# A loop written out: TensorE's stream in a routed expert stage of 79 slots

## The reference, cut to what matters

```python
logits = xt @ Wg.T + bg
top_vals, top_idx = jax.lax.top_k(logits, 2)
rw = softmax(top_vals)
gu = einsum('th,ehf->tef', xt, Wgu) + bgu        # per expert 256 -> 512
gate, up = minimum(gu[..., ::2], 7), clip(gu[..., 1::2], -7, 7)
gated = (up + 1) * gate * sigmoid(1.702 * gate)
out_e = einsum('tef,efh->teh', gated, Wd) + bd   # per expert 256 -> 256
out = einsum('teh,te->th', out_e, onehot(top_idx, rw))
```

## Time and profile before

| | |
|---|---|
| median of three runs | 772.86 us (769.19 to 773.58) |
| the profiled execution | 767.49 us |
| its span, first to last instruction | 765.7 us |
| TensorE busy, share of the span | 613.7 us, 80% |
| weight loads | 314.6 us, 41% |
| VectorE | 488.7 us, 64% |
| ScalarE | 328.9 us, 43% |
| GpSimd | 351.0 us, 46% |
| mean granted TensorE clock | 0.898 |

### The profile page before, as it was taken

One profiled execution on the slowest core, in us unless ns is written; L12 is line 12 of the kernel. 1 busy time (PEld: TensorE's weight loads), 2 busy tenths in 40 slices (PEclk: granted clock), 3 DMA queues, 4 the chain that ended last, 5 costly groups with the idle time before them and its releaser, 6 DMA issues.

```text
span 765.7 us, 13490 instructions
## 1 busy us (share of the span) xinstructions
PE 613.7 (80%) x3148; PEld 314.6 (41%) x3149; DVE 488.7 (64%) x1381; ACT 328.9 (43%) x739; POOL 351.0 (46%) x433
## 2 busy tenths in 40 slices
PE   1987888778999797979798973069999999999910
PEld 0666333523434252525252543034555555555510
DVE  5576325756487566866767644446777777777796
ACT  3854634226666464655555332013333333333331
POOL 5864623232744656467557355412333333333353
PEclk9998987679999899989899985579999999999975
DMA  9811000074000101010101011523333333333397
GB/s 321 272 11 12 0 1 0 2 270 146 1 1 12 49 2 56 4 55 0 55 1 57 1 55 56 168 55 84 91 87 88 85 87 88 86 86 88 73 377 275
DMA packets 93219, 62.37 MB, mean 81 GB/s; under 512 B 68186, under 2 KB 78558, under 8 KB 93056
## 3 DMA queue, kind: packets, MB, share of 16 engines
q1 hardware_dynamic: 85168, 44.04, 20.8%
q0 software_dynamic: 6864, 16.86, 6.5%
q10 hardware_dynamic: 1152, 1.06, 0.5%
HBM read 27.97 MB, written 25.56 MB: 70 GB/s over the span
## 4 chain that ended last, share of the span: by engine, by line
PE 51%; SPq 14%; DVE 12%; issue 9%; ACT 6%; DMA 4%; POOL 2%; another core or an unknown queue 1%; ACTq 0%; POOLq 0%; DVEq 0%
SPq L379 7%; PE bank L1037 5%; PE bank L891 4%; PE bank L866 4%; PE bank L995 3%; PE bank L1017 3%; SPq L380 3%; PE bank L855 3%; PE bank L1054 3%; PE bank L1019 3%; SPq L375 3%; PE bank L1068 2%; PE bank L1160 2%; PE bank L1161 2%; PE bank L1163 2%
## 5 line engine op out<-in xcount | busy, mean ns | idle before, releaser
L588 POOL DMA_INDIRECT y_rows<-AR x79 | 77.2, 977 | 165.4 <-ACT AR L815 161.1
L491 POOL TENSOR_TENSOR W<-STG,W 128x512 f16<-128x512 f32 (+1 forms) x48 | 56.1, 1169 | 122.2 <-ACT W L620 120.9
L804 ACT ACTIVATE AR<-AR 128x256 f32<-128x256 f32 x79 | 32.9, 417 | 160.4 <-DVE AR L1585 138.1
L1410 DVE RECIPROCAL AR<-bank 128x512 f32<-128x512 f32 x16 | 53.7, 3354 | 38.1 <-PE bank L1037 31.2
L548 POOL DMA_INDIRECT xs_rows<-AR,SLOT x64 | 63.4, 991 | 27.4 <-issue 18.1
L720 ACT ACTIVATE AR<-bank 128x512 f32<-128x512 f32 (+1 forms) x80 | 47.6, 596 | 51.9 <-PE bank L1023 47.9
L1396 DVE TENSOR_REDUCE MX<-bank 128x4 f32<-128x308 f32 x128 | 56.6, 475 | 18.4 <-PE bank L995 13.8
L1585 DVE TENSOR_SCALAR AR<-bank 128x256 f32<-128x256 f32 x79 | 33.5, 424 | 51.5 <-PE bank L1163 47.9
L1160 PE MATMUL bank<-W,AR 128*128 x158 | 61.3, 388 | 0.0
L1161 PE MATMUL bank<-W,AR 128*128 x158 | 61.1, 387 | 0.0
L995 PE MATMUL bank<-KCUR,AR 128*128 (+1 forms) x128 | 41.9, 329 | 19.4 <-DVE MX L1396 10.0
(11 more groups left out here) (229 smaller groups left out, 1443.6 us busy)
## 6 DMA issues: line engine op xcount, KB each, us to landing
W<-in_wexp SPq DMA_DIRECT2D x16, 768.0 KB, 5.3
W<-y_rows SPq DMA_DIRECT2D x8, 1024.0 KB, 15.3
X<-in_x SPq DMA_DIRECT2D x4, 1024.0 KB, 11.9
out<-X SPq DMA_DIRECT2D x8, 512.0 KB, 8.1
CST<-in_cst SPq DMA_DIRECT2D x1, 1309.0 KB, 8.4
AR<-xs_rows SPq DMA_TRANSPOSE x79
AR<-xs_rows SPq DMA_DIRECT2D x79, 1.0 KB
y_rows<-AR POOLq DMA_INDIRECT x79
```

The source lines that it names most:

```text
L491: pool.tensor_tensor(w[:, 1], STG[:, q], w[:, 0], ALU.subtract).then_inc(s["w_split"], 1)
L588: pool.indirect_dma_start(y_rows, bass.IndirectOffsetOnAxis(ap=NIX[:, k:k + 1], axis=0), CY[:, k, :], None, bounds_check=TOPK * NTOK - 1, ...
L1410: dve.reciprocal(AT[:, m], DEN[:, :]).then_inc(s["rec_s"], 1)
```

## The change: what it does

TensorE's loop in the expert stage is written out in Python: 79 times `c_tg`, `c_down`, `c_gu` with n a constant, so all waits compare with constants. Each `c_down` and each `c_gu` fetches its expert number with an `expert(n)` of its own, which stands directly ahead of it. `QUAD` is still made but no longer read. Two waits go, in `c_gu` for `cu_r` and in `c_tg` for `cgl_r`; both are implied by other waits ahead of them on TensorE. The other engines' instructions stay as they are.

```diff
             def c_gu(n, k, t, e):
                 q = k % 2
-                if not isinstance(n, int) or n >= 2:
-                    pe.wait_ge(s["cu_r"], n - 1)
                 pe.wait_ge(XTIN[k], 16 * (t + 1))
...
             def c_tg(n, q):
                 pe.wait_ge(s["cgd_r"], n + 1)
-                if not isinstance(n, int) or n >= 2:
-                    pe.wait_ge(s["cgl_r"], n - 1)
                 for c in range(DC):
...
-            def steps(n, t, k, u):
-
-                four = pe.value_load(QUAD[0:1, ds(t, 1)], min_val=0, max_val=NEXP ** 4 - 1)
-                c_tg(n + 1, 1)
-                c_down(n, 0, four % NEXP)
-                c_gu(n + 3, (k + 3) % IN, u + (k + 3) // IN, four // NEXP ** 2 % NEXP)
-                c_tg(n + 2, 0)
-                c_down(n + 1, 1, four // NEXP % NEXP)
-                c_gu(n + 4, k, u + 1, four // NEXP ** 3)
-
-            steps(0, 0, 0, 0)
-            with pe.Fori(0, (NSLOT - 7) // IN) as t:
-                steps(t * IN + 2, t * 2 + 1, 2, t)
-                steps(t * IN + 4, t * 2 + 2, 0, t + 1)
-            c_tg(NSLOT - 4, 1)
-            c_down(NSLOT - 5, 0, expert(NSLOT - 5))
-            c_gu(NSLOT - 2, (NSLOT - 2) % IN, (NSLOT - 2) // IN, expert(NSLOT - 2))
...
+            for n in range(3):
+                c_gu(n, n % IN, n // IN, expert(n))
+                if n == 1:
+                    c_tg(0, 0)
+            for n in range(NSLOT):
+                if n + 1 < NSLOT:
+                    c_tg(n + 1, (n + 1) % 2)
+                c_down(n, n % 2, expert(n))
+                if n + 3 < NSLOT:
+                    c_gu(n + 3, (n + 3) % IN, (n + 3) // IN, expert(n + 3))
```

## The result

The changed kernel takes 798.19 us (median of four runs, 796.96 to 802.15) against 771.03 us (768.92 to 773.58) of the kernel before, run beside it: a ratio of 1.036, 95% interval 1.031 to 1.041. It is slower, as forecast (790.6 us, range 782 to 801), and 7.6 us above the forecast value. The profiled execution took 796.96 us, its span is 795.2 us, 29.5 us more than before.

The account below looks back on a forecast made before the run. It took SyncE's 2.86 us a slot as the floor under the expert stage. Held loads add 17.4 us up to slot 74, then +0.6 and -0.3 at the end: 772.86 + 17.7 = 790.6 us, range 782 to 801.

Parts of the forecast that it names:

- What bounds the kernel: Expert stage before the change: SyncE's transposing loads, 2.86 us a slot, are the floor; a quicker TensorE gains nearly nothing.
- The load is held at the wait: `c_down`'s register load starts only when `c_tg`'s wait for `cgd_r` ends, so `c_down` starts 0.77 us after the release.
- The cycle of two slots: TensorE's expert stage: 2.65 + 0.77 + 1.25 + 1.51 = 6.18 us per two slots, taken as 3.08 us a slot.
- the third term: From the start of `c_down` to the start of `c_gu`: 1.30 us less 0.051 for a dropped wait, 1.25 us.
- the other form that it named: Slots alternate, one long (3.5 us) and the next short (2.7 us), with the same sum for the pair.
- TensorE's busy share: In the expert stage of the changed profile, TensorE would be busy near 2.6 of 3.1 us a slot.
- The start: Slot 7 finds its rows and full clock; counted from slot 1's transposes at 510.81, its `c_gu` starts at 525.15 us.
- The end: Slot 74 to the final additions takes 17.7 us instead of 17.1, +0.6; a wait for `y_rows`' second read goes, -0.3.
- The loads hide: Rival at the wait for `cgd_r`: loads are covered, SyncE's pace holds, about 772.7 us; chance 0.06.
- The clock dips: Rival: TensorE, busy less, runs at 0.93 of the clock in the stage, +7.6 us, about 798 us; chance 0.06.
- Code fetches stall TensorE: Rival: fetching written-out code, 12 to 24 more packets, stalls TensorE 1 us each, 803 to 815 us; chance 0.07.
- The sum: Whole kernel: 17.4 + 0.6 - 0.3 = +17.7 us, giving 790.6 us; own range 785 to 797.

Follow-up runs that it names:

- written-out one with packed numbers: Changed kernel's written-out stream and dropped waits, but with the packed `QUAD` load of every second slot, ahead of `c_tg`: 775.46 us, ratio 1.004.
- The placements: Four variants of the changed kernel with `c_down`'s load, `c_gu`'s load, both, or a single load a slot placed ahead of `c_tg`: ratios between 1.003 and 1.010.
- one load ahead: Changed kernel with one expert load a slot, ahead of `c_tg`, kept in a register from `c_gu` to the same slot's `c_down`: 776.02 us, ratio 1.003.
- constant numbers: Changed kernel with each slot's expert a fixed constant, so no register loads and no routing's choice of weights: 771.24 us, ratio 0.997.
- the kernel with the pause: Changed kernel, with VectorE waiting before its second group of final additions until GpSimd has issued its last scatter: 798.80 us, ratio 1.036.

## Why the prediction was right, and where it was not

**What bounds the kernel: right.** The bound named, SyncE's 2.86 us a slot, is confirmed by taking it away: 2.70 us. The busy share of TensorE (97% of the window in the earlier trace rows) would have said otherwise: matmul lengths overlap (in the earlier trace rows one of 0.38 us starts at 724.54 and the next at 724.76), so a short wait between two need not show as idle time. That this hid the waits for rows is inferred: those listed from slot 8 to 74 are 1.3 us in all, while slot 7 to 74 gained 8.8 us with SyncE written out, about 1.4 of it in the step to slot 8.

**The load is held at the wait: right.** The load starts at 644.6, with the release at 644.61, as the earlier trace rows had it at 720.9 and 727.2. Moving the loads ahead of the wait, with nothing else changed, takes 1.036 to 1.008. This was the step on which the forecast stood. In the traces of the four written-out kernels with `c_down`'s load behind the transposes it starts within 0.01 us of their weight load in about every second slot (32 to 34 times between 525 and 735 us).

**The cycle of two slots: right in form, 0.09 us short.** Forecast 2.65 + 0.77 + 1.25 + 1.51 = 6.18, cut to 6.16. Averaged over the 32 long slots from slot 11 to 74, with the 1.52 of the short ones, it is 2.66 + 0.75 + 1.35 + 1.52 = 6.28. Only the third term, from `c_down` to `c_gu`, was mis-sized, 1.25 for 1.35: I took one case from the earlier trace rows, in which the load takes 0.31 us, and subtracted a wait from it. A load there is not always 0.30 us; over these slots:

```profile
L1147 PEldq TENSOR_LOAD <-AR x133: 296/303/523, 531.6 to 738.8; - x133
```

In the long slots the load ahead of `c_gu` takes 0.43 us on average, and all the others take 0.30 to 0.31; why is open. The three loads of the earlier trace rows showed nothing of it. 3.13 instead of 3.08 us a slot is 3.3 us over 67 slots. The sequencer is not stuck in every slot, as the working had it first, but in every second one (33 of 67), the other form that it named. TensorE's busy share was misjudged: 173.41 of 192 us is 2.83 us of 3.13, not near 2.6.

**The start: partly right.** Slot 7 indeed found its rows, and there was no low clock: 1.00 in the window from 524 us, where before had 0.57. But the stage began later: the first `c_gu` at 503.39 instead of 502.92 us, the second at 507.36 instead of 505.88, after waiting 0.81 us for its rows, and the granted clock was 0.50 from 504 to 508 us and 0.59 to 512, where before had 0.57 and 1.00. So the transposes of slot 1, from which the forecast counted, start at 513.02 instead of 510.81; from there to slot 7 it is 14.5 us, against 14.3 in the forecast. The start of the stage scatters from profile to profile (slot 7 starts at 519.9 to 531.0 us over the kernels here), so the 3.0 us can't be laid to the change.

**The end: mis-sized.** Forecast +0.6 and -0.3, measured +2.7 and +3.7. The first read of `y_rows` starts 743.34 - 737.1 = 6.2 us behind slot 74's `c_gu`, where before it was 725.32 - 714.1 = 11.2, so more of the scatters run beside the reads, and one takes 6.07 us to land. I had counted the earlier reads only as a gain. The rest is the scatter of 16.11 us. It does not follow from additions that run without a pause: before had a scatter of 1.22 us that starts behind the pause and runs beside further additions,

```profile
733.90 2.14 DVE L1639 SCALAR_TENSOR_TENSOR X<-W,RW,X 128x256 f32<-128x256 f32 x4 [0.30 <-DMA W<-y_rows]
```

```profile
734.40 1.22 POOL L588 DMA_INDIRECT y_rows<-AR  x1 [0.35 <-DVE X L1639]
```

and the last section has kernels with no pause at all and a short scatter. What decides is open.

**The rivals.** *The loads hide*: no; it needs the release less than about 2.0 us after `c_gu`, and it was 2.66. *The clock dips*: no, 1.00 throughout. *Code fetches stall TensorE*: the count was right and the place was not. Queue 8 on the page of the changed kernel:

```profile
q8 instruction: 27, 0.44, 0.2%
```

12 packets more than in the earlier trace rows, the low end of my 12 to 24, but no idle time of 1 us on TensorE: the longest "issue" ahead of the two loads' users is 0.4 us. Their price appears elsewhere, in the last section.

**The sum.** The span grew by 29.5 us, 11.8 more than the 17.7 forecast: 2.3 at the start, 3.3 in the cycle, 2.1 and 4.0 at the end, to rounding. All four are of one sign. By the medians, in which the profiled start counts less, the growth is 27.2 us, 9.5 more than forecast, and the forecast's own range, up to 3.16 us a slot, just misses 798.19; the whole range held it only through the 3 us added for the spread of the runs. Of the misses only the cycle's is a size in the mechanism that was forecast; the start and the long scatter differ from trace to trace without a cause found here, so that the sum ended inside the range is in part luck.

## What to carry to other kernels

A register load inside TensorE's stream added no listed wait here while the sequencer was ahead (642.3 for a matmul at 642.94), and 0.54 us where it stood behind a wait that held (`c_down` 0.76 us behind the transposes instead of 0.22); with the loads moved the ratio fell from 1.036 to between 1.003 and 1.010. Put it ahead of the last wait that the engine is expected to sit in, or keep the value from an earlier use. Before speeding up the busiest engine, compare its period with that of the queue that feeds it: here 0.17 us a slot in SyncE's list was worth 1%, with TensorE's code untouched. Before you explain a difference at the end of a kernel, look at that place in every trace you have: here the same scatter took about 1 us in eleven kernels and 16 us in three.

## What the runs showed of the hardware that was not expected

**Long issues on SyncE fall together with code fetches.** Queue 8 is named "instruction" in the profile, and its packets are taken for fetches of code. Between 525 and 700 us the kernels whose TensorE stream is written out fetch code 8 to 12 times, about every 17 us; those with the loop not at all, or once. SyncE's issue times, same stretch (530 to 700 us), for the kernel before with SyncE written out (loop on TensorE) and for the written-out one with packed numbers:

```profile
L379 SPq DMA_TRANSPOSE AR<-xs_rows x64: 1207/1213/1300, 529.6 to 699.3; - x64
```

```profile
L379 SPq DMA_TRANSPOSE AR<-xs_rows x59: 1052/1212/1944, 529.6 to 698.3; - x59
```

Issues of L379 over 1.35 us and of L380 over 0.6 us between 525 and 700 us: 73 in the ten kernels with TensorE's stream written out, and 72 of them start within 0.8 us of a packet of queue 8; in the four looped ones there are two, one of them at such a packet. One long issue, of the written-out kernel with packed numbers, with its slot, and the queue's row for 578 to 581 us:

```profile
578.46 0.39 PE L1156 MATMUL bank<-BEX,AR 128*128 128x512 f16 x1
578.53 1.87 SPq L379 DMA_TRANSPOSE AR<-xs_rows  x1
580.60 0.42 SPq L380 DMA_DIRECT2D AR<-xs_rows  x1
581.64 0.39 PE L1156 MATMUL bank<-BEX,AR 128*128 128x512 f16 x1 [0.52 <-DMA AR<-xs_rows]
```

```profile
q8 instruction: 1, 0.02, 2.0%
```

The issue takes 1.87 instead of 1.21 us, and TensorE later waits for rows. Where SyncE is the limit this can count in full: that kernel's seven long issues are 3.5 us over 1.21 each in 525 to 700 us, and its period is 2.90 - 2.83 = 0.07 us above that of before, 4.9 us over 67 slots. The placements bear on this too. Over the same stretch their long issues exceed 1.21 and 0.42 us by 2.7 us in all with one load ahead, 5.7 with `c_gu`'s moved, 6.3 with `c_down`'s, 6.1 with both, and 1.0 with constant numbers, at 2.87, 2.95, 2.92, 2.99 and 2.83 us a slot: a part of the differences among them may be this, and not the loads. With SyncE's list written out there is slack, and 7.4 us of waiting for rows in 9 pieces is what is left of it on TensorE. That the fetch causes the long issue is inferred from the coincidence; no run changed the fetches alone.

**GpSimd's last scatter takes about 1 us or 16 us beside the same additions.** Six kernels here run VectorE's additions without a pause from the first one up to the last scatter. In three of them (changed; `c_gu`'s load moved; before with SyncE written out) it takes 16.11, 15.93 and 15.93 us and ends 0.8 to 0.9 us after the last addition; in the other three (waits put back; both loads ahead; loop with one load per use) it takes 1.26, 1.03 and 1.10 us. GpSimd, then VectorE, with the waits put back:

```profile
766.58 1.26 POOL L588 DMA_INDIRECT y_rows<-AR  x1 [0.30 <-issue]
```

```profile
765.33 1.66 DVE L1619 SCALAR_TENSOR_TENSOR X<-W,RW,X 128x256 f32<-128x256 f32 x4
766.92 1.34 DVE L1623 SCALAR_TENSOR_TENSOR X<-W,RW,X 128x256 f32<-128x256 f32 x2
```

From the first addition to the end of the span it is 38.3 us in the three with the long scatter, and 34.3 to 36.3 us in the eleven others. What decides is open. Beside GpSimd's additions VectorE needs 3.30 us a group in the kernel with the pause, against 2.38 us in the changed kernel, where none of them run beside it; no run shows whether this and the length of the scatter have one cause.
